# Other prices for changes of tiling, and another table of due-time shifts, in the planner of a causal-attention and mixture-of-experts kernel

## What is computed

```python
x = x + attn(layernorm(x))
x = x + ffn(layernorm(x))

def attn(x):                              # B, S, E = 8, 1024, 256
    Q, K, V = (x @ W + b for W, b in ...) # 16 heads of 16
    logits = where(causal, Q @ K.T * 16 ** -0.5, -inf)
    h = layernorm(x @ dp_w1 + dp_b1) * ln_g + ln_b
    drift = gelu(h) @ dp_w2 + dp_b2
    gate = tanh(gelu(drift * g_w1 + g_b1) @ g_w2 + g_b2)
    return (softmax(logits) * gate) @ V @ Wo + bo

def ffn(x):                               # 8 experts of width 128
    scores = sigmoid(x @ gate_w.T)        # the 2 best groups of 4, then the 2 best experts
    y = sum(weight_e * (silu(x @ w1_e.T) * (x @ w3_e.T)) @ w2_e.T for the 2 chosen e)
    return y + (silu(x @ sg.T) * (x @ su.T)) @ sd.T
```

## Time and profile before

| | |
|---|---|
| median of 3 runs | 1799.14 us (1796.13 to 1805.52) |
| the profiled execution | 1808.59 us, of which the span from first to last instruction is 1806.6 us |
| PE busy (matmuls) | 1653.0 us, 91% of the span, 12785 matmuls |
| DVE busy | 1292.4 us, 72% |
| ACT busy | 1081.9 us, 60% |
| POOL busy | 811.8 us, 45% |
| matmuls that only keep PE busy | 135, 42.9 us |
| DMA | 261 MB, mean 145 GB/s |

### The profile page before, as it was taken

How to read it: one execution, slowest core, us unless ns; L and a number is a source line. 1 busy time by engine, 2 the same in 40 slices (tenths; PEclk the granted TensorE clock), 3 DMA queues, 4 the chain that set the end, 5 groups by cost and what they waited for, 6 DMA issues and landing times.

```text
span 1806.6 us, 34673 instructions
## 1 busy us (share of the span) xinstructions
PE 1653.0 (91%) x12785; PEld 982.5 (54%) x12785; DVE 1292.4 (72%) x2528; ACT 1081.9 (60%) x1808; POOL 811.8 (45%) x1390
## 2 busy tenths in 40 slices
PE   7798989989988999899998989999999889999888
PEld 3344446435544566455654555555564557666677
DVE  5776767967795777777785757877688666963655
ACT  3466756665655655675656755586556765568432
POOL 5234533463345221632237863363207773157760
PEclk9699999999998999999998999999999999999999
DMA  5556655554445532644545665453535675336440
GB/s 151 158 156 194 176 169 152 182 153 124 125 127 147 158 104 87 174 113 120 159 118 151 185 194 152 127 162 108 147 93 172 198 197 159 97 129 199 135 122 13
DMA packets 192708, 261.25 MB, mean 145 GB/s; under 512 B 19616, under 2 KB 127264, under 8 KB 192544
## 3 DMA queue, kind: packets, MB, share of 16 engines
q1 hardware_dynamic: 181792, 229.67, 44.0%
q0 software_dynamic: 10752, 29.37, 5.6%
HBM read 130.98 MB, written 127.40 MB: 143 GB/s over the span
## 4 chain that ended last, share of the span: by engine, by line
PE 54%; DVE 14%; DMA 8%; ACT 8%; POOL 8%; issue 5%; SPq 3%; another core or an unknown queue 0%; POOLq 0%; ACTq 0%; DVEq 0%
PE ps_all L1961 10%; PE ps_all L2071 10%; DVE mx L1549 7%; PE ps_all L1941 6%; PE ps_all L1908 6%; PE ps_all L2102 5%; PE ps_all L1892 4%; ACT probs L1358 4%; PE ps_all L1878 3%; PE ps_all L1970 3%; POOL xs_s L1207 2%; PE ps_all L2081 2%; PE ps_all L2034 1%; DMA rr<-r_s 1%; DMA out<-rr 1%
## 5 line engine op out<-in xcount | busy, mean ns | idle before, releaser
L1549 DVE TENSOR_REDUCE mx<-ps_all 128x2 f32<-128x1024 f32 (+2 forms) x640 | 619.0, 1006 | 132.5 <-PE ps_all L1908 74.4
L1358 ACT ACTIVATE probs<-ps_all 128x1024 f32<-128x1024 f32 x576 | 571.8, 1028 | 218.0 <-PE ps_all L1941 209.9
L1175 POOL TENSOR_SCALAR_AFFINE_SELECT probs<-probs 128x256 f32<-128x256 f32 (+1 forms) x448 | 190.9, 443 | 495.5 <-ACT probs L1358 491.3
L1961 PE MATMUL ps_all<-probs,vaug 128*32 128x512 f32 (+3 forms) x3072 | 319.4, 516 | 21.9 <-POOL probs L1175 15.3
L1908 PE MATMUL ps_all<-k_st,q_st 63*128 63x512 f32 (+3 forms) x1536 | 269.3, 401 | 48.0 <-ACT probs L1358 16.3
L1941 PE MATMUL ps_all<-q_st,k_st 64*128 64x512 f32 (+3 forms) x1536 | 265.6, 401 | 29.3 <-ACT probs L1358 9.9
L1908 PEld LDWEIGHTS ps_all<-k_st,q_st 63*128 63x128 f32 x1536 | 135.1, 193 | 163.7 <-issue 52.2
L1941 PEld LDWEIGHTS ps_all<-q_st,k_st 64*128 64x128 f32 x1536 | 130.9, 191 | 158.9 <-issue 67.2
L2071 PE MATMUL ps_all<-w_hi,x2h 128*128 128x512 f32 (+1 forms) x480 | 168.2, 350 | 4.3 <-DVE x2l L1598 2.5
L1804 DVE SCALAR_TENSOR_TENSOR act_t<-act_t,ps_all 128x256 f32<-128x256 f32 x168 | 70.4, 419 | 123.4 <-ACT act_t L1421 110.9
L2071 PE MATMUL ps_all<-w_lo,x2h 128*128 128x512 f32 (+1 forms) x480 | 157.0, 327 | 0.0
(11 more groups left out here) (195 smaller groups left out, 2849.8 us busy)
## 6 DMA issues: line engine op xcount, KB each, us to landing
qk_s<-qh SPq DMA_DIRECT2D x116, 256.0 KB
q_st<-qk_s SPq DMA_DIRECT2D x128, 192.0 KB
k_st<-qk_s SPq DMA_DIRECT2D x128, 192.0 KB
xs<-xs_s SPq DMA_DIRECT2D x72, 256.0 KB
ys_s<-ysb SPq DMA_DIRECT2D x72, 256.0 KB
o_s<-o_sb SPq DMA_DIRECT2D x64, 256.0 KB
qk_s<-ql SPq DMA_DIRECT2D x57, 256.0 KB
xs_s<-ysb SPq DMA_DIRECT2D x20, 512.0 KB, 6.0
```

Of the source, the lines that this page charges most:

```text
L1175: last = nc.gpsimd.affine_select(out=block, in_=block, compare_op=ALU.is_ge, fill=0.0, base=0, pattern=[[0, heads], [1, P]], channel_multi ...
L1358: nc.scalar.activation(to, of, ACT.Exp, scale=DH ** -0.5).then_inc(freed[release[item][0]], 1)
L1549: last = nc.vector.tensor_reduce(to[:, :, p, qt % QPC], both[:, :, at:at + keys], X_AXIS, ALU.max)
L1961: last = mm(bank(first)[32 * h:32 * h + 32, q0 - c * CHUNK:], vaug[:, kt, g, h * VW:h * VW + 32], probs[:, s % 2, h, at:at + cols], start= ...
```

## The change

The constants of the planner are others, its rule for the duration of a PE item is another, and the table of shifts has 75 kinds in place of 40. Before, a change of tiling cost 190 ns, or 100 ns into `PV`, and an item of the same tiling cost up to 90 ns more only if PE had been idle ahead of it. Now a change costs 130 ns whatever the tiling, and every other item but `PV` and `ED` costs 60 ns more. The handicap for another tiling falls from 12,000 to 7,000 ns. No instruction of the computation is added, removed or made larger.

```diff
-SWITCH, EXPOSED = 100, 90
+SWITCH, EXPOSED = 130, 60
...
-SAME_TILING = 12000
+SAME_TILING = 7000
...
-LATER = {"AC": 8000, "AQ": -1000, "AX": 7000, "CB": 6000, "CC": -41000, "CG": 3000, "CJ": 2000, "CL": -8000,
...
-         "XL": 5000, "XO": -1000, "XT": -10000, "YC": 12000, "YS": 22000}
+LATER = {"AB": -3000, "AC": 25000, "AE": 16000, "AG": -27000, "AN": 2000, "AQ": -1000, "AR": 21000, "AS": 37000,
...
+         "WL": -19000, "WP": -26000, "XH": 3000, "XL": 27000, "XO": 30000, "XT": -6000, "XZ": -35000, "YC": -21000,
+         "YS": 10000}
...
                 if tile != tiling:
-                    ns += SWITCH + EXPOSED * (tile != COLS)
-                    tiling = tile
-                elif idle and tile != COLS:
-                    ns += min(EXPOSED, idle)
+                    ns, tiling = ns + SWITCH, tile
+                elif item[0] not in ("PV", "ED"):
+                    ns += EXPOSED
```

## The result

| | before | changed |
|---|---|---|
| median | 1802.46 us (20 runs, 1790.13 to 1809.33) | 1808.70 us (20 runs, 1805.00 to 1824.49) |
| the profiled execution | 1808.59 us, span 1806.6 | 1806.74 us, span 1804.9 |

The ratio is 1.0055 with a 95% interval of 1.0036 to 1.0074: slower by a little over half a percent, where 1% faster was forecast, and just outside the range. Two later comparisons, on chips numbered 14 and 4, gave 0.9976 (0.9955 to 0.9997) and 0.9989 (0.9967 to 1.0010). So the change lies between a quarter of a percent faster and half a percent slower from one comparison to the next; in none was it 1% faster. Each chip was used on one occasion, so whether the chip or the occasion makes the difference is not shown.

The account below looks back on a forecast made before the run. PE's own work, many short waits and the clock were taken to bound the kernel. The terms +16 - 18 - 14 + 3 - 4 = -17 us gave 1782 us against the median of 1799.1, range 1757 to 1808.

Parts of the forecast that it names:

- Part 1: On PE, changes of tiling rise by 138, from 996 to 1134; +16 us, bounds 12 and 26.
- Part 2: PE's waits for PSUM banks held by exponentials and maxima get fewer; -18 us, ends 0 and -50.
- part 3: On PE, 65 of 135 filling matmuls go, two thirds of their time gained; -14 us, bounds 0 and -20.7.
- The count of short distances: Under 1.0 us of PE work before the next `M` or `QK` wants a bank: 114 cases before, 73 after; -20 us.
- Part 4: Chains of an expert unit: `HT` follows its `EU` at under 1.5 us in 14 cases, not 2; +3 us, bounds 0 and +6.
- Part 5: PE's clock outside the start: less waiting takes 8% off the 52 us lost in its falls; -4 us.
- Rival C: Fewer filling matmuls let PE's clock fall more often, so slower, 1818 us with twelve more falls; chance 0.15.
- Costed at nothing: Full-tiling runs, POOL's order, SP's DMAs, PE's work before the first scores and after the last `PV`: no change in time.
- a sign of being wrong altogether: The start to 77 us, or last `PV` to the end, differs by more than 5 us; the sum had nothing.
- Rival B: Gain eaten: tiling changes +26, filling only filled waits, 0, bank waits -13; about 1799 us, chance 0.22.
- rival D: The whole gain, -46 us: banks -30, filling -20.7, clock -10, changes and chains +15; 1753 us, chance 0.10.

Follow-up runs that it names:

- the two bare kernels: The kernel before and the changed kernel, orders untouched, with none of their filling matmuls issued; medians 1795.6 and 1787.4 us on the same chip.
- table_only: The kernel before with the new table of shifts and the handicap of 7,000, its old prices and rule kept; 0.9914 of the kernel before.
- The nudged kernel: The changed kernel with 131 ns in place of 130 for a change of tiling; 1.0137 of the kernel before.
- changed_more_fill: The changed kernel, order untouched, with 158 filling matmuls in place of 70; 0.9995 of the kernel before.
- The nudged kernels: Kernels with 1 ns more in one price: before 1.0153; changed 1.0137; changed with handicap 12,000 1.0069 and 1.0070; before with new table and handicap 7,000 0.9944 and 0.9920.

## Why the prediction was wrong

**What bounds the kernel** was read rightly: PE's work, many short waits, and the clock. All variants move in these three.

**Part 1, changes of tiling, +16.** The price is confirmed where it can be read, 0.34 us behind a `PV` as before. PE's busy time other than filling rose by 17.3 us at an equal clock, and by 15.8 between the two bare kernels, so the size of the term came out. But that the changes of tiling make it is not shown, and the agreement is in part luck: table_only, with 111 changes more than before, has 1600.5 us of such time at a clock of 0.970, and the changed kernel, with only 27 more than that, 1613.3 at the same clock. As a predictor of the time the count is worthless here: 931 changes gave 1.0248, 1107 gave 0.9914.

**Part 2, waits for banks, -18,** failed together with part 3, which is the step that was wrong. The count of short distances was right in direction. Between the bare kernels the four rows fall from 72.2 to 45.4 us, by 26.8. Between the kernels with filling they fall from 50.4 to 46.6, 41.4 or 38.5, by 4 to 12, because 21.8 us of the old order's waits lay under its filling. The sum took the same waits twice, once as waits and once as filling. Parts 2, 3 and 4 together were to bring -29; filling and idle time together went down by 19.0 in the two profiled executions.

The length of a wait was the other weakness. I had priced each at the mean of 0.48 us and taken short distances as the only cause. The longest in the four rows is 1.9 us before, and 3.9, 4.1 and 3.0 in the three executions of the changed kernel; that such waits come from inputs late in the queues of ACT or DVE is likely, but was not followed up. The nudged kernel shows how little the count says: 78 cases of `M` and `QK` under 1.0 us of distance against 73 in the changed kernel, counted in the same way, and 44.5 us in the four rows, less than the first trace of the changed kernel has, and yet it ran at 1.0137 on chip 5.

**Part 3, filling matmuls, -14. This is the step that failed.** It took two thirds of the filling for time that PE could have used. If that were so, the kernel before without its 42.9 us of filling would have been some 29 us faster. It was 0.34% slower, 6 us. In one trace of each, 26.9 of the 42.9 us came back as idle time, which leaves about a third of the filling exposed and not two thirds, and the clock fell by 0.012 besides. What the change takes away was worth its time: in place of -14 the term is about +6 for the filling of the old order, and nothing to -3 for that of the new one, whose removal left it at 0.9991 beside 0.9976 and 0.9989 on other chips. The row that I rested on the earlier trace rows was misread. No idle time of PE follows the pair, but the weights of the `QK` behind it were not loaded ahead of it, as those of the `M` before the pair were, by 0.12 us. By the trace their loading (PEld) waited for a reduction of DVE that began at 1126.26 us, took 1.22, and so ended just as the pair did:

```profile
1127.53 0.19 PEld L1941 LDWEIGHTS ps_all<-q_st,k_st 64*128 64x128 f32 x2 [0.56 <-DVE mx L1549]
```

**Part 4, expert units, +3.** PE's idle time ahead of the transposes is 9.9 us, where the same group had 4.3 before: +5.6, near the upper bound of 6. A term that the sum did not have is as large: ahead of the turned maxima (`MT`) PE is idle for 11.9 us in place of 5.8, and for 10.8 and 12.6 in the executions on chips 14 and 4.

**Part 5, the clock, -4.** In the two profiled executions it was equal, 0.962. Over the runs of chips 14 and 4 the changed kernel lies 0.0045 and 0.002 below before, 8 and 4 us the other way. In the 20 runs of the first comparison the longest goes with the lowest clock (1824.49 us, 0.952), though one at 0.960 took 1821.82. Rival C's mechanism may therefore have been at work, at a small part of its price. But it is no cause by itself: changed_more_fill won the clock back and not the time.

**Costed at nothing.** The start was rightly so: the first scores begin 0.2 us later. The end was not: the same work took 10 us less in the profiled execution, about 8 of them by the clock (134.6 x 0.06). The prediction named that as a sign of being wrong altogether, and it was, though this one went in favour of the change. DMA waits were not looked at, and rose in the chain from 8 to 11%.

**How far that closes the account.** The orders alone are worth -8 us, where the sum without part 3 had -3. The old order's filling, +6, and the new one's, 0 to -3, make it -2 to -5 us; chips 14 and 4 show -4 and -2. Each of these numbers is uncertain by some 4 us. The first comparison, +6 us, lies 12 to 14 us above the two others, and nothing here explains that; the clock of the kernel before is not on record for its 20 runs.

**The chances.** Rival B (eaten up, about 1799) is what chips 14 and 4 show, and the first comparison lies between B and C. B was right that the filling stood in waits, and it came to its number with changes of tiling at 0.19 us each, +26, where PE's other busy time rose by 17. In rival D, half of 46 us less is 1776 us, not 1765. Beside the step that failed there is a second error, in the range: I summed five differences of some 10 us from counts, for a change that deals the whole order anew. The nudged kernels now show what that alone does to the time, a spread of 1 to 2%, and no term of my sum carried it. That a forecast so made came within 1.5% of the time says little for its terms. The range should have been about 1780 to 1830, and the chance of faster under one half.

## What to carry to other kernels

Where a planner orders thousands of items greedily, any constant deals a new order, and the time of one order says little of the rule behind it: nudge the constant by a meaningless amount two or three times, before and after, and compare families. If the kernel one starts from turns out to be the fastest of its family, the change has to beat that luck as well. Prices for such a planner are better read apart for items that waited and items that did not, since an average over both hides the difference that the order depends on; no run here tested it.

Work that fills a wait and the wait itself are one quantity. Whoever forecasts that both shrink should price them together, and a variant of each kernel without the filling shows what the orders alone are worth.

## What the runs showed of the hardware that was not expected

The same pair of programs compared differently from one chip and occasion to the next: 1.0055, 0.9976 and 0.9989, with intervals of 0.002 each way, while another program compared alike on two (0.9873 and 0.9882). The kernel before itself has medians from 1790.1 to 1802.5 us on different chips.

The granted clock of one program varies from run to run, and the time with it: 0.963 at 1805.0 us and 0.952 at 1824.5 for the changed kernel, some 1.8 us per thousandth between these two, which is what the span times a thousandth gives. Not every run lies on that line: one at 0.960 took 1821.8. Matmuls that compute nothing can buy the clock back (0.9645 to 0.9705 for 88 of them), but here no time came of it that could be told.
